# A 4-bit dequantisation's divisions and products moved from GpSimd to ScalarE in 64-column blocks, with padding rows zeroed by DMA and a re-spread schedule

## The reference, cut to what is computed

```python
x = layernorm(x + attention(x, wq, bq, wk, bk, wv, bv))
x = layernorm(x + ffn(x, w1, w2, w3))
# attention: 32 heads of 16 features, softmax over the HEADS of one token
#   scores = einsum('bshd,bstd->bsht', q, k) / 4 ; probs = softmax(scores, -1)
#   context = einsum('bsht,bstd->bshd', probs, v)
# ffn: w1, w2 are 1376 x 512, w3 is 512 x 1376; each is first quantised and dequantised:
#   per block of 64 values: absmax, normalise, nearest of 16 codes, times absmax
#   y = (silu(x @ dq1.T) * (x @ dq2.T)) @ dq3.T
```

## Time and profile before

| what | value |
|---|---|
| median of 3 runs | 797.81 us (794.51 to 806.0) |
| the profiled execution | 802.0 us, its span 800.2 us |
| busy share of the span | PE 91%, DVE 81%, ACT 59%, POOL 15% |
| mean granted TensorE clock | 0.851 of full speed |
| projections, attention, feed-forward | to about 166 us, to about 381 us, to the end |
| moved by DMA | 116.22 MB, mean 145 GB/s |

### The profile page before, as it was taken

One profiled execution on the slowest core, in us unless ns is written; L12 is line 12 of the kernel. 1 busy time (PEld: TensorE's weight loads), 2 busy tenths in 40 slices (PEclk: granted clock), 3 DMA queues, 4 the chain that ended last, 5 costly groups with the idle time before them and its releaser, 6 DMA issues.

```text
span 800.2 us, 14244 instructions
## 1 busy us (share of the span) xinstructions
PE 731.4 (91%) x5668; PEld 624.6 (78%) x5668; DVE 648.1 (81%) x896; ACT 475.7 (59%) x629; POOL 116.8 (15%) x95
## 2 busy tenths in 40 slices
PE   4899999937989999999899989898999999999983
PEld 4778788837989999998677868787888888788761
DVE  2799999999897997986569699999897586765386
ACT  3688989855645636455546577676664456642124
POOL 2011104242101111010102021121111010100022
PEclk9999999975555655555899999999999999999995
DMA  9965445899957995947203631201414101250347
GB/s 223 228 165 162 147 148 171 216 295 242 245 126 182 253 256 151 282 123 269 100 1 135 210 133 53 81 27 55 122 66 158 48 2 34 74 195 12 115 149 157
DMA packets 89330, 116.22 MB, mean 145 GB/s; under 512 B 24720, under 2 KB 70800, under 8 KB 86448
## 3 DMA queue, kind: packets, MB, share of 16 engines
q1 hardware_dynamic: 88128, 113.21, 50.2%
q10 hardware_dynamic: 1136, 2.10, 1.2%
HBM read 76.42 MB, written 38.86 MB: 144 GB/s over the span
## 4 chain that ended last, share of the span: by engine, by line
PE 49%; DVE 23%; issue 10%; ACT 8%; DMA 6%; SPq 2%; POOL 2%; DVEq 0%; POOLq 0%; ACTq 0%
DVE nf_acc L1079 11%; PE ps_p L960 10%; PE ps_s L879 6%; PE ps_s L878 6%; PE ps_s L877 6%; ACT nf_y L724 5%; PE ps_p L877 5%; PE ps_p L879 5%; PE ps_p L878 5%; PE ps_s L947 3%; PE ps_t L898 2%; DMA qk_parts<-qk_p 2%; DMA dequantised<-nf_acc 2%; DVE nf_acc L1075 1%; PE ps_t L902 1%
## 5 line engine op out<-in xcount | busy, mean ns | idle before, releaser
L1079 DVE SCALAR_TENSOR_TENSOR nf_acc<-nf_y,nf_acc 128x1024 f32<-128x1024 f32 (+4 forms) x266 | 306.5, 1152 | 31.6 <-ACT nf_y L724 22.0
L724 ACT ACTIVATE nf_y<-nf_w,bound_b 128x1024 f32<-128x1024 f32 (+4 forms) x285 | 289.7, 1048 | 21.0 <-DVE nf_acc L1079 10.7
L960 PE MATMUL ps_p<-probT,v_bd 128*68 128x32 f32 x1024 | 125.5, 302 | 4.5 <-DVE probT L1128 4.5
L960 PEld LDWEIGHTS ps_p<-probT,v_bd 128*68 128x68 f32 x1024 | 122.7, 211 | 5.8 <-issue 3.2
L643 POOL TENSOR_TENSOR nf_w<-nf_w,nf_rec 128x1024 f32<-128x1024 f32 (+4 forms) x19 | 38.9, 2048 | 346.3 <-DVE nf_rec L1063 346.3
L1234 DVE TENSOR_TENSOR silu<-silu,ps_s 128x512 f32<-128x512 f32 (+1 forms) x44 | 30.1, 684 | 71.5 <-PE ps_s L879 71.4
L877 PE MATMUL ps_p<-x_hl,w_hl 128*128 128x512 f32 x192 | 77.5, 404 | 5.4 <-DVE w_hl L1097 3.4
L879 PE MATMUL ps_p<-x_hl,w_hl 128*128 128x512 f32 x192 | 75.8, 395 | 0.0
L877 PE MATMUL ps_s<-x_hl,f_ha 128*128 128x512 f32 x192 | 75.7, 394 | 0.0
L879 PE MATMUL ps_s<-x_hl,f_la 128*128 128x512 f32 x192 | 75.6, 394 | 0.0
L878 PE MATMUL ps_s<-x_hl,f_ha 128*128 128x512 f32 x192 | 75.5, 393 | 0.0
(11 more groups left out here) (100 smaller groups left out, 1259.2 us busy)
## 6 DMA issues: line engine op xcount, KB each, us to landing
x_hl<-x_parts SPq DMA_DIRECT2D x10, 2048.0 KB, 8.6
qk_parts<-qk_p SPq DMA_DIRECT2D x64, 204.0 KB, 2.5
q_st<-qk_parts SPq DMA_DIRECT2D x48, 272.0 KB, 6.6
k_st<-qk_parts SPq DMA_DIRECT2D x48, 272.0 KB, 7.5
x_parts<-x_st SPq DMA_DIRECT2D x16, 512.0 KB, 4.5
nf_w<-in_L_ffn_w SPq DMA_DIRECT2D x24, 256.0 KB, 3.2
dequantised<-nf_acc SPq DMA_DIRECT2D x10, 512.0 KB, 2.8
v_blocks<-v_t SPq DMA_DIRECT2D x16, 256.0 KB, 3.3
```

The source lines that it names most:

```text
L724: act.activation(nf_y[0:p, at % NY, 0:w], nf_w[0:p, u % 2, 0:w], ACT.Identity, bias=bound_b[0:p, i:i + 1], scale=STEEP).then_inc(s_ny, 1)
L960: t = pe.matmul(ps_p[0:MV, (G + 3) % NPV, i * H:(i + 1) * H], v_bd[hb % 2][:, :, g * GI + i], probT[:, G % 2, i], start=True, stop=True)
L1079: dve.scalar_tensor_tensor(out=acc, in0=y, scalar=float(NF4[i + 1]), in1=acc, op0=ALU.min, op1=ALU.max).then_inc(s_nacc, 1)
```

## The change

1. `normalise` and `scale` are no longer one POOL instruction a unit. ACT does them with one ACTIVATE (Identity, scale taken from a column of the tile of reciprocals or maxima) per block of 64 columns, 16 for a unit of 1,024. Each is cut into two halves, placed before the ramps of levels 11 and 13 of the unit before (`normalise`) and of levels 3 and 5 of the unit after (`scale`). The first unit's `normalise` stands in front of the first tau.
2. The stacks' padding rows alone are zeroed, by two DMAs of 32 rows of 17,408 bytes per slot: slot 0 from the still-zero `v_bd[0]`, slot 1 from slot 0's zero rows. They are issued by SP ahead of the stack loads; POOL sets the ones of `v_bd[0]` only when the first two have landed, and PE's first scores of each half block wait for them too.
3. `v_bd` is cleared in four memsets of 1,088 columns instead of one of 4,352.
4. FIRST_LOAD goes from tau 39 to tau 37.
5. Attention gets six levels more, five new levels stand between attention and feed-forward (`LV_T`), and the feed-forward stage gets eleven fewer, with none of its early steps above four. The last block's ct and xt turns move one or two steps back, out of the steps that hold the "f" turns of the first group.
6. A unit counts as finished six levels later, which moves stores, reloads and "f" turns.

```diff
-    FIRST_LOAD = 3 * KC * (NBK - 1) + 3
+    FIRST_LOAD = 3 * KC * (NBK - 1) + 1
...
-        LV_A[8 * b + 10:8 * b + 13] = [1, 1, 1]
-    LV_F = [(1, 2)] * 4 + [(2, 2)] + [(1, 2)] * 2 + [(2, 3)] * 8 + [(2, 2)] * (FIRST_OF[2] - 15) + [(3, 3)] * 6
+        LV_A[8 * b + 10:8 * b + 13] = [2, 1, 2]
+    LV_T = (2, 3)
+    LV_F = [(1, 2)] * 2 + [(1, 1)] * 2 + [(1, 2)] + [(2, 2)] * (FIRST_OF[2] - 5) + [(3, 4)] * 3 + [(3, 3)] * 2 + [(0, 1)]
...
-    F_TURNS = {0: [("f", W_UNITS[2], 0), ("f", W_UNITS[2], 1), CT_LAST[0]],
-               1: [("f", W_UNITS[3], 0), ("f", W_UNITS[3], 1), CT_LAST[1]],
-               2: CT_LAST[2:4], 3: CT_LAST[4:], 5: XT_LAST[:2], 6: XT_LAST[2:]}
-    MOMENTS_F, NORM_F = 3, 4
+    F_TURNS = {0: [("f", W_UNITS[2], 0), ("f", W_UNITS[2], 1)], 1: [("f", W_UNITS[3], 0), ("f", W_UNITS[3], 1)],
+               2: CT_LAST[:2], 3: CT_LAST[2:4], 4: CT_LAST[4:], 6: XT_LAST[:2], 7: XT_LAST[2:]}
+    MOMENTS_F, NORM_F = 4, 5
...
-        while len(finished) < NU and done >= LEVELS * (len(finished) + 1):
+        while len(finished) < NU and done >= min(LEVELS * (len(finished) + 1) + 6, LEVELS * NU):
...
                 if tau == FIRST_LOAD:
+                    sp.wait_ge(s_proj, 3 * KC * (NBK - 1))
+                    sp.wait_ge(s_vzero[0], Q4)
+                    for st in st_0:
+                        sp.dma_start(st[3::4].rearrange("r h t -> r (h t)"),
+                                     v_bd_0[3::4].rearrange("r m t -> r (m t)").bitcast(BF16)).then_inc(s_szero[0], 16)
                     parts_stored(sp, 2 * KC)
-                    sp.wait_ge(s_szero, 2)
                     load_stacks(sp, 0)
                     values_stored(sp, KC)
-                    sp.wait_ge(s_vzero, 1 + Q4)
+                    sp.wait_ge(s_vzero[0], 2 * Q4)
                     load_v(0)
-            sp.wait_ge(s_szero, 4)
+            sp.wait_ge(s_proj, 3 * KC * NBK)
+            sp.wait_ge(s_szero[0], 16 * 2)
+            for st, zero in zip(st_1, st_0):
+                sp.dma_start(st[3::4].rearrange("r h t -> r (h t)"), zero[3::4].rearrange("r h t -> r (h t)")
+                             ).then_inc(s_szero[1], 16)
             load_stacks(sp, 1)
...
-                pool.memset(v_bd[slot][:], 0.0).then_inc(s_vzero, 1)
+                for q in range(Q4):
+                    pool.memset(v_bd[slot][:, DV * q:DV * q + DV], 0.0).then_inc(s_vzero[slot], 1)
...
+            def normalise(u, part):
+                p, nb = parts_of(u), width(u) // QBLOCK
+                act.wait_ge(s_nrec, u + 1)
+                for k in range(nb * part // 2, nb * (part + 1) // 2):
+                    v = nf_w[0:p, u % 2, QBLOCK * k:QBLOCK * k + QBLOCK]
+                    t = act.activation(v, v, ACT.Identity, scale=nf_rec[0:p, k:k + 1])
+                if part:
+                    t.then_inc(s_nnorm, 1)
+            def scale(u, part):
+                p, nb = parts_of(u), width(u) // QBLOCK
+                act.wait_ge(s_nacc, LEVELS * (u + 1))
+                for k in range(nb * part // 2, nb * (part + 1) // 2):
+                    acc = nf_acc[0:p, u % 2, QBLOCK * k:QBLOCK * k + QBLOCK]
+                    t = act.activation(acc, acc, ACT.Identity, scale=nf_max[0:p, u % 2, k:k + 1])
+                if part:
+                    t.then_inc(s_dq, 1)
             def steep(n):
                 for at in range(level[0], min(level[0] + n, LEVELS * NU)):
                     u, i = divmod(at, LEVELS)
                     p, w = parts_of(u), width(u)
+                    if i in (3, 5) and u:
+                        scale(u - 1, int(i == 5))
+                    if i in (11, 13) and u + 1 < NU:
+                        normalise(u + 1, int(i == 13))
...
+            for k in range(2):
+                normalise(0, k)
             act.wait_ge(s_const, LEVELS + 1)
...
             context(GG - 2)
+            steep(LV_T[0])
             for key in TAIL_2:
                 high(key)
             context(GG - 1)
+            steep(LV_T[1])
...
                 if g == 0:
+                    pe.wait_ge(s_szero[hb % 2], 16 * 2)
                     pe.wait_ge(s_ldq[hb % 2], 16 * 6 * (hb // 2 + 1))
```

More of the change, by code:

```diff
@@ L195, in layer_kernel @@
         if g == 1:
-            back = max(back, 8 if kind == "t" else 4)
+            back = max(back, 9 if kind == "t" else 5)
         else:
@@ L286, in layer_kernel @@
         s_const = sem("s_const")
-        s_vzero = sem("s_vzero")
-        s_szero = sem("s_szero")
+        s_vzero = [sem(f"s_vzero{i}") for i in range(2)]
+        s_szero = [sem(f"s_szero{i}") for i in range(2)]
         s_pad = sem("s_pad")
@@ L330, in layer_kernel @@
         s_dq = sem("s_dq")
-        s_dst = sem("s_dst")
+        s_dst = [sem(f"s_dst{i}") for i in range(2)]
         s_rld = [sem(f"s_rld{u}") for u in range(NU)]
@@ L595, in store_out @@
                     sp.dma_start(of[t0:t0 + TI, :], part[TI * e:TI * e + TI, Q4 * b + q]).then_inc(s_out, 16)
+            levels(sum(LV_T))
             load_x1(0)
@@ L635, in _ @@
             pool.wait_ge(s_const, LEVELS + 1)
[L637 to L661, removed]
-                level[0] = min(level[0] + n, LEVELS * NU)
             def clear(slot):
                 if slot:
-                    pool.wait_ge(s_vzero, 1 + Q4)
                     pool.wait_ge(s_ql, 2 * KC * NBK)
@@ L671, in clear, with ones @@
                     values_stored(pool, KC * NBK)
-                pool.memset(v_bd[slot][:], 0.0).then_inc(s_vzero, 1)
-                pool.wait_ge(s_vzero, (1 + Q4) * slot + 1)
                 for q in range(Q4):
-                    pool.memset(v_bd[slot][32 * q:32 * q + 32, DV * q + D], 1.0).then_inc(s_vzero, 1)
-                pool.wait_ge(s_vzero, (1 + Q4) * (slot + 1))
-            def clear_stacks(slot):
-                if slot:
-                    pool.wait_ge(s_proj, 3 * KC * NBK)
-                else:
-                    pool.wait_ge(s_proj, 3 * KC * (NBK - 1))
-                for st in stacks[slot]:
-                    pool.memset(st[:].bitcast(F32), 0.0).then_inc(s_szero, 1)
-            clear(0)
-            normalise(0)
-            for tau in range(3 * KC * NBK):
-                if tau == 3 * KC * (NBK - 1):
-                    clear_stacks(0)
-                around(LV_P[tau])
-            clear_stacks(1)
-            clear(1)
-            for G in range(GG):
-                around(LV_A[G] // 2)
-                if G in MOMENTS_AT:
-                    b = MOMENTS_AT[G]
-                    pool.wait_ge(s_ve, b + 1)
-                    pool.tensor_tensor(rstd[:], ve[:], half_neg[:], ALU.pow).then_inc(s_rstd, 1)
-                around(LV_A[G] - LV_A[G] // 2)
-            for s in range(NS):
-                around(LV_F[s][0])
-                if s == MOMENTS_F:
-                    pool.wait_ge(s_ve, NBK)
-                    pool.tensor_tensor(rstd[:], ve[:], half_neg[:], ALU.pow).then_inc(s_rstd, 1)
-                around(LV_F[s][1])
+                    pool.memset(v_bd[slot][:, DV * q:DV * q + DV], 0.0).then_inc(s_vzero[slot], 1)
+            def ones(slot):
+                pool.wait_ge(s_vzero[slot], Q4)
+                for q in range(Q4):
+                    pool.memset(v_bd[slot][32 * q:32 * q + 32, DV * q + D], 1.0).then_inc(s_vzero[slot], 1)
+                pool.wait_ge(s_vzero[slot], 2 * Q4)
+            clear(0)
+            pool.wait_ge(s_szero[0], 16 * 2)
+            ones(0)
+            clear(1)
+            ones(1)
+            for b in range(NBK):
+                pool.wait_ge(s_ve, b + 1)
+                pool.tensor_tensor(rstd[:], ve[:], half_neg[:], ALU.pow).then_inc(s_rstd, 1)
             for n in range(Q4 * NBK):
@@ L1198, in _ @@
             swap(GG - 1)
-            for key in TAIL_1 + TAIL_2:
+            for key in TAIL_1:
                 low(key)
+            lift(LV_T[0])
+            for key in TAIL_2:
+                low(key)
+            lift(LV_T[1])
             def drain(n):
```

26 lines of the change are left out of this document (15 added, 11 removed).

## The result

The changed kernel takes 837.13 us (median of 4 runs, 836.31 to 838.16), the kernel before 798.38 in the runs beside it. The ratio of the two is 1.047, 95% interval [1.040, 1.055]: slower, where I forecast no change that can be measured. The profiled execution has a span of 836.3 us, 36.1 more than before.

A forecast was written before the change was run, and what follows sets the result against it. Bound: no clear engine in projections, PE in attention, DVE in the first 17 feed-forward steps, PE in later ones. 6.3 + 2.6 + 1 + 1.5 - 14 - 1.6 = -4.2 us from 797.81 gave 794 us, range 779 to 813.

The forecast's parts named there:

- Price of a block: On ACT, one 64-column block of a division or product pass costs 0.234 us, 126 us more over all units.
- the slower rival: The default offset travels as a second operand, a block costs 0.322 us, total 811 us; chance 0.15.
- ACT waits 2 us (0 to 5): Late projections: the earlier load delays stores, so ACT's high part of tau 42 waits 2 us for a qk_p slot.
- Projections, "13.1 us": Projections: 137 blocks, 32 us of ACT work, lengthen the four blocks by 2, 2.7, 3.6 and 4.8 us.
- L1075, "8.8 (8.5 to 9.77)": First seam: the one-tile DVE level of 9.77 us, held while POOL clears the stacks, gets 8.8 us shorter.
- their loads are first needed four steps into attention ... I cost them at nothing (0 to 4): Early attention: loads of the second slot's stacks, queued behind two more zero DMAs, cost nothing, at most 4 us.
- the early part: Early attention: three exposed half passes cost 5.6 us, DVE no longer stalled by POOL gives 3.0 back, net 2.6.
- The six levels, "+1 (-4 to +5)": Attention: six more levels, 7.7 us of DVE, go into DVE's idle time and cost 1 us.
- The end, "+1.5": End of attention: five levels fall into 3.46 us of ACT idle time with one half pass, costing 1.5 us.
- Feed-forward, "-14": The first 17 feed-forward steps get 14 us shorter (19 to 7): at most 20, less 6 us of stalls.
- The eighth moves to step 17: Feed-forward: the eighth "f" turn pair leaves the first 17 steps for step 17, with no cost counted there.
- The reload stall, "-1.6": Feed-forward beyond the 17 steps: the second of two PE stalls at a unit's reload goes, saving 1.6 us.

The follow-up runs named there:

- experiment 6: The changed kernel with only 2 of the 16 blocks of each pass divided or multiplied, the rest left out; 797.06 us, 0.994 of the kernel before.
- experiment 3: The changed kernel with divisions and products back on GpSimd, one instruction a unit; 803.68 us, 1.003 of the kernel before.
- Experiment 1: The changed kernel with FIRST_LOAD back from tau 37 to tau 39; 826.47 us, 1.033 of the kernel before.
- experiment 5: The changed kernel with divisions and products on GpSimd, FIRST_LOAD at tau 39, a unit finished with its last level; 794.15 us, 0.991 of the kernel before.
- number 10: The kernel before with the changed lists and ScalarE's divisions and products in blocks, seams and FIRST_LOAD as before; 824.21 us, 1.028 of the kernel before.
- number 8: The kernel before with only the change's lists of levels, turns and moments, and the norm one step later; 791.20 us, 0.987 of the kernel before.
- Experiment 2: The changed kernel with three levels moved from feed-forward steps 32-34 to 12-14, putting unit 11's f turn in step 16; 833.76 us, 1.041 of the kernel before.

## Why the prediction was wrong, step by step

- **Price of a block: right.** 0.240 us against 0.234. The forecast thus failed in its own case, not in one of the rivals; the slower rival's 811 needed 0.322. The Trainium skill, "Perfetto Trace Analysis", section "Optimizing Scalar/DVE Operations", says that grouping work can help when an engine is saturated. No run here groups the blocks; experiment 6, which leaves most of them out and wins 40 us, shows only that their time counts. The 0.147 us that I had estimated from that section's overhead was too low.
- **"ACT waits 2 us (0 to 5)" for the slot: wrong, 13.76 us, 14.95 in experiment 3.** This is the largest single error. I had ACT wanting the slot 14 us after the pause begins, SP free after 13.5, and a store that lands at once. It is 9.9, 14.7 (157.88 to 172.56) and 9 us. SP's place in its list trails ACT's, as it stores a tile only when DVE has finished it, and the first store behind the loads takes SP 4.34 us to issue, where the median of the 16 store issues from 150 to 200 us is 0.49. Experiment 1 settles it: two taus later, no wait.
- **Projections, "13.1 us": too small, about 21.** The 9th, 17th and 25th high part start at 71.34, 109.90 and 150.70, before at 64.59, 100.27 and 134.99. So the first block loses 6.75 us (said 2), the second 2.9 (2.7), the third 6.1 (3.6), and what is left for the last is 25.6 - 15.7 - 13.8 + 9.0 = 5.1 (4.8). The first block's step fails because ACT, ahead of its first tau, waits 4.94 us for the reciprocals and then divides a whole unit. In the third I added up ACT's time and left out what PE waits for: the 4.56 us for x at the block's end, and the 4.4 us at half clock behind it. The waits of ACT for PE did go there, but for 1.7 us. In experiments 3 and 6 PE waits under 1 us for a split x, and the first maximum comes 20 and 22 us earlier.
- **L1075, "8.8 (8.5 to 9.77)": right as a length, wrong as a gain.** It is 0.73 us now. But the step "their loads are first needed four steps into attention ... I cost them at nothing (0 to 4)" fails: in experiment 5 the whole gain is lost by the fifth maximum. Behind a late ACT the level takes only 3.58 us anyhow (10), and number 1, with zero rows by DMA, has its first maximum just 2.8 us ahead of number 10's: loss and gain lay over each other, and I added them.
- **Attention: the early part right, the lists wrong.** Number 10 against number 8 shows the passes step by step. Steps 0, 3 and 4 grow by 1.9, 1.9 and 2.2 us (said: three by 1.87), and the steps in which POOL had held DVE up lose 1.6 and 1.35 (said 3.0): net 3.0 against 2.6. The other steps cost another 2.7, of which 2.0 lie in steps 11, 19 and 27, whose passes I let hide beside context turns. The six levels, "+1 (-4 to +5)", cost 5.1 (184.6 from the first to the last maximum before, 189.7 in number 8), the top of the range. The end, "+1.5", takes 4.9: 3.1 by the five levels and 1.9 by the half pass.
- **Feed-forward, "-14": right, and its parts nearly so.** The lists alone give -20.8 (8), just beyond my limit of 20, and the passes take 5.9 (10 against 8, whose 17 steps hold one "f" turn more) to 8.4 (the change against 3) back, where I had left 6.
- **"The eighth moves to step 17" at no cost: wrong, 9.8 us.** I took the turn's work out of the 17 steps and did not ask who needs it in step 17. Experiment 2 shows the cause.
- **The reload stall, "-1.6": -1.7, by luck.** I placed the second of the two stalls beyond the 17 steps. In PE's timeline of the kernel before it stands ahead of silu 17 (553.80):

```profile
547.20 1.07 PE L916 MATMUL ps_t<-ident,f_lb 128*128 128x128 f32 x8 [2.62 <-DMA f_lb<-dequantised]
```

Number 8 has neither stall, and from silu 18 to 43 it takes 210.63 us against 210.75 before. The gain is that GpSimd's product no longer holds DVE up. Two levels in DVE's timelines, in number 3, whose turns stand as in the changed kernel (a product begins there at 689.44), and in the changed kernel:

```profile
689.67 2.48 DVE L1091 SCALAR_TENSOR_TENSOR nf_acc<-nf_y,nf_acc 128x256 f32<-128x256 f32 x2
```
```profile
726.21 0.96 DVE L1077 SCALAR_TENSOR_TENSOR nf_acc<-nf_y,nf_acc 128x256 f32<-128x256 f32 x2
```

Number 3 takes 1.55 us longer from silu 18 to 43, these 1.5; number 6, without these products too, has 209.08.

## What to carry to other kernels

A moved list entry has a producer and a first consumer: look up both before it is costed at nothing, above all where it lands in the consumer's own step. Before crediting a stall that goes, look two or three events on for what comes in next (here the loads behind it in one DMA queue) and credit only the gain at that event. An engine's idle time hides new work only where the work does not stand in order ahead of what another engine waits for: ACT was idle for 41% of the span, and yet 27 us (number 10 against 8, less the turn's 9.7) to 35 us (the change against 3) of its 137 us of blocks came out in the total; leaving out 111 us of them won 40 (experiment 6).

## What I had not expected of the hardware

PE's clock answered a single gap of 5.87 us at once: 1.00 in the stretch before it, 0.50 in the 5.3 us after it, then 1.00 again. Behind the 4.56 us that end at 145.61 it was 0.50 as well, for 4.4 us.

And a one-tile level of 1,088 columns on DVE takes 0.73 us with no POOL work beside it, but one that starts just behind POOL work ends only about 0.6 us after that work: 2.43 us behind a product that ends at 167.48 (experiment 5), 9.78 behind a product and two memsets of the stacks, which end at 173.99 (experiment 8).

```profile
165.56 1.92 POOL L661 TENSOR_TENSOR nf_acc<-nf_acc,nf_max 128x1024 f32<-128x1024 f32 x1 [9.36 <-DVE nf_acc L1091]
```
```profile
165.63 2.43 DVE L1087 TENSOR_SCALAR nf_acc<-nf_y 128x1088 f32<-128x1088 f32 x1
```

A level that starts first is not held: one of 1,024 columns at 65.10 us of the kernel before takes 0.69, with a product from 65.26 on.
